# Three weight pieces of the attention start loaded later, and the second feed-forward quad's unpacking in another order

## The reference

```python
x = _layernorm(x + attention(x, w_qkv, w_o))     # 16 heads of 32, causal, softmax
x = _layernorm(x + ffn(x, gate, up, down))       # MLP_DIM = 4096
# ffn, weights given as 4-bit codes, two in each int, and scales of blocks of 32
Wg, Wu, Wd = (dequant_nvfp4(codes, scales) for each)
out = (gelu(xt @ Wg.T) * (xt @ Wu.T)) @ Wd.T
```

## Time and profile before

| | |
|---|---|
| time, median of 3 runs | 2676.31 us (2674.91 to 2676.31) |
| profiled execution | 2674.77 us, of them 2672.9 us span |
| PE busy | 2612.9 us, 98% |
| DVE, ACT, POOL busy | 1739.2, 1154.1, 1044.4 us |
| granted TensorE clock, mean | 0.991 |
| DMA | 530.43 MB, mean 198 GB/s |

### The profile page before, as it was taken

One profiled execution on the slowest core, in us unless ns is written; L12 is line 12 of the kernel. 1 busy time (PEld: TensorE's weight loads), 2 busy tenths in 40 slices (PEclk: granted clock), 3 DMA queues, 4 the chain that ended last, 5 costly groups with the idle time before them and its releaser, 6 DMA issues.

```text
span 2672.9 us, 41044 instructions
## 1 busy us (share of the span) xinstructions
PE 2612.9 (98%) x14322; PEld 2177.0 (81%) x14322; DVE 1739.2 (65%) x3504; ACT 1154.1 (43%) x2616; POOL 1044.4 (39%) x1160
## 2 busy tenths in 40 slices
PE   7999999999789999999999999999999999999998
PEld 6777887778468888888888888788888888888887
DVE  5777777777779888886333333655555575555656
ACT  4666666666644444443233323323333342333332
POOL 1444434443634444333444444523223242323333
PEclk9999999999799999999999999999999999999999
DMA  8676876778466665566555554466555546555552
GB/s 249 183 186 172 218 212 171 191 194 227 112 228 229 216 223 209 203 235 244 214 205 187 218 201 174 175 231 247 170 181 203 191 170 228 211 180 181 192 203 75
DMA packets 180061, 530.43 MB, mean 198 GB/s; under 512 B 14480, under 2 KB 72976, under 8 KB 157072
## 3 DMA queue, kind: packets, MB, share of 16 engines
q1 hardware_dynamic: 179856, 527.82, 59.6%
HBM read 378.86 MB, written 148.90 MB: 197 GB/s over the span
## 4 chain that ended last, share of the span: by engine, by line
PE 70%; DVE 2%; DMA 1%; issue 1%; POOL 0%; ACT 0%; SPq 0%; POOLq 0%; DVEq 0%; ACTq 0%
PE bank L1140 23%; PE bank L1141 23%; PE bank L1142 23%; PE bank L452 0%; PE bank L438 0%; DVE acc L1647 0%; DMA x1T_scratch<-x_late 0%; DMA scale<-down_scales 0%; DVE bx_l L1598 0%; DVE bstats L1788 0%; POOL probs L743 0%; DMA wd<-w_scratch 0%; DVE hid L1750 0%; PE bank L419 0%; PE bank L462 0%
## 5 line engine op out<-in xcount | busy, mean ns | idle before, releaser
L743 POOL TENSOR_SCALAR probs<-probs,row_inv 128x128 f32<-128x128 f32 (+3 forms) x512 | 263.0, 533 | 366.2 <-DVE row_inv L664 366.2
L1955 POOL TENSOR_TENSOR inter_l<-hid,inter_h 128x512 fp32r<-128x512 f32 x144 | 192.9, 1340 | 540.9 <-ACT inter_h L1316 540.8
L1140 PE MATMUL bank<-bx_h,wg 128*128 128x512 f32 x896 | 350.9, 392 | 1.0 <-ACT u_g L1316 1.0
L1141 PE MATMUL bank<-bx_l,wg 128*128 128x512 f32 x896 | 350.3, 391 | 0.0
L1140 PE MATMUL bank<-bx_h,wu 128*128 128x512 f32 x896 | 349.4, 390 | 0.0
L1141 PE MATMUL bank<-bx_l,wu 128*128 128x512 f32 x896 | 349.2, 390 | 0.0
L1142 PE MATMUL bank<-bx_h,wu 128*128 128x512 f32 x896 | 348.6, 389 | 0.0
L1142 PE MATMUL bank<-bx_h,wg 128*128 128x512 f32 x896 | 348.6, 389 | 0.0
L1750 DVE TENSOR_TENSOR hid<-hid,bank 128x512 f32<-128x512 f32 x192 | 131.9, 687 | 299.4 <-PE bank L1142 298.3
L1657 DVE TENSOR_TENSOR acc<-acc,bank 128x512 f32<-128x512 f32 x392 | 263.4, 684 | 94.3 <-PE bank L1142 84.3
L1960 POOL TENSOR_TENSOR inter_l<-hid,inter_h 128x512 fp32r<-128x512 f32 x112 | 146.0, 1303 | 368.6 <-ACT inter_h L1316 368.6
(11 more groups left out here) (173 smaller groups left out, 6015.0 us busy)
## 6 DMA issues: line engine op xcount, KB each, us to landing
wg<-w_scratch SPq DMA_DIRECT2D x48, 1792.0 KB, 9.2
wu<-w_scratch SPq DMA_DIRECT2D x48, 1792.0 KB, 13.1
q_st<-qk_scratch SPq DMA_DIRECT2D x128, 256.0 KB, 5.0
k_st<-qk_scratch SPq DMA_DIRECT2D x128, 256.0 KB, 7.0
w_scratch<-wg SPq DMA_DIRECT2D x16, 1792.0 KB, 8.2
w_scratch<-wu SPq DMA_DIRECT2D x16, 1792.0 KB, 10.6
b_slot<-t_scratch SPq DMA_DIRECT2D x112, 256.0 KB, 3.4
b_slot<-w_scratch SPq DMA_DIRECT2D x84, 256.0 KB, 2.8
```

The lines of the kernel that those rows point to most:

```text
L743: pool.tensor_scalar(p, p, row_inv[:, h % 4, k:k + 1], 1.0, ALU.mult, ALU.mult).then_inc(norm_done, 1)
L1140: pe.matmul(out, a(0), b(0), start=start, stop=False, skip_group_check=True)
L1141: pe.matmul(out, a(0), b(1), start=False, stop=False, skip_group_check=True)
L1955: pool.tensor_tensor(inter[1][:, m, t, :], hid[:, 2 * m + t, :], f32(inter[0][:, m, t, :]), ALU.subtract).then_inc(inter_split, 1)
```

## The change

Pieces 5, 6 and 7 are issued by SP behind the reads of the second stacks instead of at the start, and split at the start of slots 3, 5 and 6 of batch 0 instead of between the first projections. In quad 1, unit 7 is spread before the second product's bank is taken, its bits are unpacked before the split of quad 2's gate weight, and its scaling comes behind addition 1; unit 8 is loaded in `start(31)`, ahead of the last waits on the attention's stores, and is unpacked behind addition 4 instead of before addition 2.

```diff
+    LATE_PIECES = {3: 5, 5: 6, 6: 7}
@@ SP, before slot 0
-            for i in range(1, len(PIECES)):
+            for i in range(1, 5):
                 load_w(i)
...
                     read_stack(1, c)
+                    if c:
+                        for i in range(5, len(PIECES)):
+                            load_w(i)
@@ ACT and DVE, before slot 0
-                if use + 3 < len(PIECES):
+                if use < 2:
                     w_part(use + 3)
@@ ACT and DVE, body
                 for s in range(SLOTS):
+                    if b == 0 and s in LATE_PIECES:
+                        w_part(LATE_PIECES[s])
@@ feed-forward, SP
+            if n == 31:
+                load_unit(8)
...
-                        if k + 5 < UNITS * NG:
+                        if 8 < k + 5 < UNITS * NG:
                             load_unit(k + 5)
@@ feed-forward, ACT
+                if j == 1:
+                    spread(7)
+                    take_u2(j, "g")
                 if prep:
                     sums_high(j + 1, 0)
-                take_u2(j, "g")
+                if j > 1:
+                    take_u2(j, "g")
...
                 split_high(j - 1, 0, 1)
-                if j == 1:
-                    spread(7)
@@ feed-forward, DVE
                     down_low(j)
+                if j == 1:
+                    unpack_bits(k + 1)
                 if prep:
                     gate_up_low(j + 1, 0)
...
                 add_down(j - 1, 1)
                 if j == 1:
-                    unpack(k + 1)
-                if prep:
+                    unpack_scale(k + 1)
+                elif prep:
                     unpack_bits(k + 2)
                 add_down(j - 1, 2)
-                if prep:
+                if prep and j > 1:
                     unpack_scale(k + 2)
...
                 add_down(j - 1, 4)
+                if j == 1:
+                    unpack(k + 2)
                 times_up(j, 1, 0)
```

## The result

| | before | after |
|---|---|---|
| time, median of 9 runs each | 2674.83 us (2673.87 to 2676.31) | 2681.95 us (2680.18 to 2684.56) |
| span of the profiled execution | 2672.9 us | 2679.1 us |
| PE busy | 2612.9 us | 2614.8 us |
| granted TensorE clock, mean | 0.991 | 0.990 |

The ratio is 1.0030, with a 95% interval of 1.0021 to 1.0038; the medians are 7.1 us apart. The forecast was 2679.2 with a range of 2672.5 to 2685. The time is in the range, 2.8 us above the forecast; "within 0.2%" was called likeliest (0.66), and what came is slower by 0.3% (0.28). The change itself was missed by more than the time: the sum had +3.7, and it is +7.1. With nine runs in place of three the median of before is 2674.83 and not 2676.31, and that hides 1.5 us.

What follows compares the result with a forecast made beforehand. PE's work (busy 2612.9 of 2672.9 us), half-clock stretches and some 60 us idle bound the kernel. Part A +6.0 and part B -2.3 gave +3.7: 2678.5 on the profiled execution, 2680.0 on the median; forecast 2679.2, range 2672.5 to 2685.

Steps and rivals of the forecast that it cites:

- the sum: Whole kernel: part A +6.0 and part B -2.3 give +3.7 us, slower.
- The start of part A: First stacks: first q write lands 3.5 us earlier, PE resumes at 30.1 instead of 33.34, with no half clock behind.
- part A: Attention's start, three weight pieces loaded and split late: 2.7 + 1.5 + 1.8 = 6.0 us slower, from 1 to 9.
- The 1.5 us for each half clock: Behind long PE waits: a clock drop costs 1.5 us, saved at the start and charged again in slot 3.
- the loss in slot 3: q2 write lands at 49.4 behind the pieces; PE resumes at 52.7 instead of 50.02, 2.7 later, plus 1.5 for the clock.
- Rival two: Slot 3: pieces don't hold the q2 write, landing about 44.8; part A +1.4, total about 2675; chance 0.15.
- Slots 5 and 6: Splits of two pieces there: 1.8 us, ACT the later engine; from 0.5 to 3.0 (DVE's whole chain).
- Part B: Second quad's new order: 2.3 us faster, from 4.2 faster to 3.3 slower; most to win 6.2.
- beside a wait DVE has anyway: Quad 1: unit 7's bits come early there, so its scaling starts at 788.85 instead of 791.01.
- rival one: Quad 2: unit 10 is the new stall, PE 3.3 later than before plus a clock drop; about 2686; chance 0.15.
- unit 10 lands beyond 811.5: Sign that the forecast is wrong; the forecast had unit 10 landing at 809.2.
- Rival three: Start: first q write lands no sooner, something other than pieces held it; +6.9, about 2683; chance 0.08.

Runs made afterwards that it cites:

- a_only: The kernel before with only the attention's part of the change, the three late pieces; 2684.49 us, ratio 1.0039.
- Experiments 9: The kernel before, pieces 6 and 7 loaded at slot 7 and split in slots 11 and 15; 2673.18 us, ratio 0.9997.
- experiment 10: e3 with the loads of pieces 6 and 7 issued behind the second stacks' reads, ahead of the q2 write; 2677.41 us, ratio 1.0014 to before.
- experiment 4, pieces_behind_k2: a_only with the three loads issued in slot 1, behind the q2 and k2 writes; 2682.14 us, ratio 1.0027 to before.
- e3: e1 with piece 7 split in slot 15 in place of 13; 2673.18 us, ratio 0.9997 to before.
- split_late, experiment 3: The kernel before, pieces 5, 6 and 7 loaded at the start but split in slots 3, 5 and 6; 2679.68 us, ratio 1.0020.
- Experiment 5: The kernel after with pieces 6 and 7 split in slots 11 and 13, staged in free space; 2680.72 us, ratio 1.0027 to before.
- e1: The kernel before, with pieces 6 and 7 loaded at slot 7 and split in slots 11 and 13; 2673.97 us, ratio 0.9999.
- Experiment 6: The kernel before with part B alone, but unit 8 unpacked behind addition 2 instead of 4; 2670.58 us, ratio 0.9985.
- 11: e3 with piece 5, still loaded early, split in slot 3; 2675.11 us, ratio 1.0006 to before.
- e4: e3 together with Experiment 6's edit, no others; 2669.20 us, ratio 0.9982 to before.

## Why the forecast was near, and where it was too low

**The start of part A was right in its mechanism, and partly by luck in its numbers.** The first q write lands at 17.4 (14.79 and 2.6; forecast 18.3), PE resumes at 30.39 (30.1) after 2.46 us (1.5), at the full clock, and the second stacks are read from 31.27 (32.4). Two misses cancel in the 30.39: the write lands 0.9 us sooner than forecast, and from the first read to PE it takes 12.9 us (30.39 less 17.48) and not 11.5. And the full clock was luck: a_only, the same program there, idles 2.48 us and goes on at half the clock (0.50 in a window from 30.9 to 34.1), and its last score of slot 0 is 2.0 us later.

**The 1.5 us for each half clock** was the author's estimate, and no run was made that shows this term alone. What the traces show in its place: from PE's first product behind the start's wait to the last score of slot 0, the same work takes 4.07 us in before and 4.04 in a_only, with the granted clock at 0.50 for the first 3.2 to 3.3 us, and 2.57 in after, at 1.00. So it was 1.5 us there; for the other half clocks it stays an estimate.

**So was the loss in slot 3.** The q2 write lands at 48.9 (49.4), PE resumes at 52.09 (52.7) after 8.28 us (about 9), and slot 4 begins at 56.06 in place of 52.16: 3.9 us, where the forecast has 2.7 + 1.5 = 4.2. Experiments 9 and 10 show that the pieces hold the write: with the same issue time but no piece ahead, it lands at 45.2, and counted from the second stacks' reads three pieces cost 4.8 to 5.1 us (forecast 4.3). All that the start wins is lost there again, and 3.0 us more. Undoing that alone doesn't save part A, as experiment 4 shows: then piece 5 is what slot 3 waits for.

**Rival two fell.** The pieces do hold the write. (Its own landing, 3.2 us before 48.3, is 45.1 and not 44.8.) From issue to landing it took 12.0 us behind three pieces (after), 8.2 without them and issued at the same time (e3), and the first q write of after took 2.6. That is what the traces show of these transfers; in what order a queue finishes its transfers in general no run tested.

**Slots 5 and 6 were mis-sized: 1.8 forecast, 3.4 measured.** From slot 4's begin to the values of head 7 after takes 15.61 us and before 13.13 (65.29 less 52.16), which is 2.5, and the values take 0.95 longer. The forecast took ACT as the later engine there (1.0 and 0.7, which is 1.7 and not 1.8). It was DVE: both its splits stand ahead of masks, and PE waits 0.42 and then 1.84 us for them. The forecast's upper bound of 3.0 named DVE's chain. The half clock behind the 1.84 us was in no term; the wait of 1.75 us before 50.02, read as one without a drop, had none indeed (1.00), as this window of before shows, so the rows of before didn't announce it. It came behind the 1.84 us in all four traces with these splits: 0.50 from 70.5 to 73.5 in after, 71.9 to 74.9 in a_only, 68.7 to 71.7 in split_late and 70.8 to 73.8 in pieces_behind_k2. Experiment 5 takes splits, wait and half clock away together.

```profile
50.00:52.60 2.60, 2.58 (x15) 2.19 (x16) 2.47 (x8) 1.68 (x6) 2.04 (x4) 1.00 0.81 253
```

**The sum was made against one execution.** The gain at the start was counted from 33.34, and the loss in slot 3 from 50.02, after a wait of 1.75 us. In two other executions of the same start the numbers are 31.97, 31.96 and, at slot 3, 2.3 to 2.4 us sooner, with waits of 0.70 us and of less than 0.3. Against the mean of the three at the sweep's wait (775.28, 772.68 and 772.89, so 773.6) after is 8.6 us late, and a_only (783.50) 9.9; against the one trace of before after is 6.9 late. Forecast: 6.0. With part B's 0.8 after's two numbers give 7.8 and 6.1, around the 7.1 measured. That the executions differ this much couldn't be seen from one trace.

**Part B was mis-sized: 2.3 us won by the forecast, 0.8 in the trace of after, 1.1 in the medians of part B alone.** What the forecast said of its end came true: the 4.71 us wait goes, and the seeds wait for unit 10. The half clock that it counted as won, 1.5 of the 6.2, stays, now behind the wait of 2.27 us (0.50 from 797.3 to 800.6). From the addition's wait (797.01; in before there is none, 788.99) to quad 2's second products it takes 23.66 us in place of 25.60, so 1.9 won. But the stretch ahead of it, from 782.18 to 797.01, takes 14.83 in place of 13.71, 1.1 lost. The forecast put unit 7's bits "beside a wait DVE has anyway", and they are: the split behind them starts when it did, 3.06 us after the split of `wd` (792.48 less 789.42; before 785.57 less 782.51). Then one instruction of it takes 1.53 us where before it took 0.42, and the addition and PE stand behind. It is so in all six traces with part B (1.52 to 1.54). Each time GpSimd begins `inter_l` 0.04 to 0.05 us ahead of it; in the eight others GpSimd begins 0.44 us behind it, and it takes 0.42. In before GpSimd's two `inter_l` run between 786.62 and 790.4, and there it is a bits instruction, at 789.30, that takes 1.67 in place of 0.69; PE doesn't wait for it. So the 1 us was there before, on an instruction that didn't matter. In quad 2 the same instruction shows both lengths under either order of quad 1, as in e1, which has no part B:

```profile
816.55 1.51 DVE L1638 TENSOR_TENSOR wg<-w_g,wg 128x256 fp32r<-128x256 f32 x1
```

```profile
816.49 1.29 POOL L1964 TENSOR_TENSOR inter_l<-hid,inter_h 128x512 fp32r<-128x512 f32 x1 [3.34 <-ACT inter_h L1325]
```

It takes 1.51 to 1.52 us in ten traces, in which GpSimd began 0.06 to 0.54 us ahead of it, and 0.41 to 0.42 in three in which GpSimd began behind it; in the last (pieces_behind_k2) GpSimd began 0.02 ahead and it took 0.42. So the extra 1.1 us goes with GpSimd having begun first. No experiment moved GpSimd alone.

How this reached the end: unit 10's load stands behind unit 8's unpacking, and that behind the addition. It was issued at 811.88; without the 6.9 us by which the sweep is late that is 805.0, and the forecast has 803.5. Its spread came 5.9 us later (forecast 5.7), and PE's second products 2.9 behind that (3.1). So the step that was off is the issue of unit 10, by 1.5 us, and 1.1 of it is the stretch above.

**Unit 10, rival one.** It was spread at 817.73. The forecast of 809.2, moved by the 6.9 us by which the sweep is late, is 816.1; the bound beyond which the rival decides is 818.4. So it stayed below, by 0.7 us; taken as it is written, without that shift, the sign "unit 10 lands beyond 811.5" was met. Experiment 6 shows how little an earlier issue gives while 3.6 MB of stores are ahead of it in the queue.

**How the loss divides, by the medians.** Queue order 4.2 (experiment 10 against 9, with two pieces), piece 5's split 1.9 (11 against 9), the splits of 6 and 7 3.2 (experiment 3's 5.1 less that 1.9; experiment 5's trace says 3.2 too), less 0.6 for what loading pieces late gives (9): 8.7, and part A alone measured 9.9. The third piece in the queue is in none of them. Part B gives back 1.1, which makes 8.8; after measured 7.1. The single intervals are some 2.4 us to each side, so the division is good to that, and no better.

**Rival three**, at 2683, came nearest in time and is not what happened: the first write did land sooner. (Its sum, +6.9, gives 2681.7 to 2683.2.)

## What to carry to other kernels

A transfer sent later must be followed to the write that it now stands ahead of: here three weight loads left the first stacks' way and took the place ahead of q2's write. PE resumed 1.6 to 3.0 us sooner at the start, and the write landed 3.7 us later. Taken away from the first projections, the splits gave back nothing that showed (in experiment 3 PE resumes at 32.96, in the three traces of before's start at 31.96 to 33.34); in slots 3, 5 and 6, ahead of the masks that PE waits for, they cost 5.1 us, a half clock among it; two of them cost nothing in slots 11 and 15, which take 7 us each with them or without. And a stall that decides a few microseconds should be seen in more than one execution before a sum is built on its size.

## What the runs showed of the hardware, unexpected

An idle of 1.84 us was followed by a granted clock of 0.50 (after, 70.2 to 73.6), and so in all four kernels with splits in slots 5 and 6; yet the idle of 2.46 us ahead of 30.39 was not (1.00 from 30.3 to 36.5). The same program went either way: at the start, after idles 2.46 us and a_only 2.48, and the first product behind takes 0.36 and 0.55 us, the clock is 1.00 and 0.50; e3 idles 2.96 and e1 2.95, again 0.36 and 0.55, with 1.00 and 0.50 from 31.3 to 34.5; in slot 3, e4 idles 2.28 and e3 2.00, 0.44 and 0.69, with 1.00 (46.8 to 50.0) and 0.50 (46.9 to 50.1). So in these traces the length of an idle didn't decide by itself.

A load issued 7.9 us sooner into a full queue (DMA share 1.03, 413 GB/s) was there 1.1 us sooner (experiment 6). One DVE instruction of 0.42 us, the 128x256 part of the split of `wg`, took 1.51 to 1.54 in 16 places of quads 1 and 2, in each of which GpSimd had begun an `inter_l` 0.04 to 0.54 us before it, and 0.41 to 0.42 in 11 in which GpSimd began after it; one place, with GpSimd 0.02 us ahead, took 0.42.
